# A fused delta-rule layer with feed-forward: the third slot's order, the place of the solve, and the engine of an add

## The reference, cut to what matters

```python
k = l2norm(silu(x @ Wk)); q = silu(x @ Wq); v = silu(x @ Wv)
log_f = log_sigmoid(x @ Wf1 @ Wf2); beta = sigmoid(x @ Wbeta) * 2.0
k_ = -beta[..., None] * k
# two steps a token: a decay step with (k_ * exp(log_f), k), and a write step with (k_, k, v, q)
def step(S, inp):
    g, a_t, b_t, k_t, v_t, q_t = inp
    bS = jnp.einsum('bhk,bhkv->bhv', b_t, S)
    S = jnp.exp(g)[..., None] * S + a_t[..., None] * bS[:, :, None, :] + k_t[..., None] * v_t[:, :, None, :]
    return (S, jnp.einsum('bhk,bhkv->bhv', q_t, S))
y = out * sigmoid(x @ Wog1 @ Wog2); y = y / sqrt(mean(y * y) + EPS) * norm_w   # per head
x = layernorm(x + y @ Wo)
x = layernorm(x + x @ W.T + b + x @ lilora_weight.T)
```

## Time and profile before

| | us |
|---|---|
| median of 3 runs | 2539.0 (2536.97 to 2541.99) |
| profiled execution | 2536.87, span 2535.0 |
| PE busy | 2121.5 (84%) |
| DVE busy | 1764.5 (70%) |
| ACT busy | 1627.2 (64%) |
| POOL busy | 838.3 (33%) |

### The profile page before, as it was taken

The page is one execution under the profiler, slowest core; times in us unless marked ns, Lnnn a source line. Parts: engine busy times, 40 slices in busy tenths (PEclk is TensorE's granted clock), DMA queues, the critical chain, the costliest instruction groups (busy, mean ns, idle before and its releaser), DMA issues.

```text
span 2535.0 us, 191611 instructions
## 1 busy us (share of the span) xinstructions
PE 2121.5 (84%) x85960; PEld 1591.0 (63%) x85960; DVE 1764.5 (70%) x4196; ACT 1627.2 (64%) x3048; POOL 838.3 (33%) x805
## 2 busy tenths in 40 slices
PE   6777888888888888888888888888888888889784
PEld 3556666666666666666666666666666666666573
DVE  3567567777766777766777766677876677776643
ACT  3656566666666666666666666666667666666554
POOL 1133233333333333323333323333333333332330
PEclk8889999999999999999999999999999999999886
DMA  3343244443344444344444344444334444433431
GB/s 100 85 120 113 90 132 136 139 130 98 120 130 139 133 129 121 105 123 138 137 131 131 96 124 136 131 139 128 111 117 124 137 137 132 130 98 120 131 111 38
DMA packets 558366, 305.46 MB, mean 120 GB/s; under 512 B 417186, under 2 KB 517152, under 8 KB 558240
## 3 DMA queue, kind: packets, MB, share of 16 engines
q1 hardware_dynamic: 558240, 304.19, 40.4%
HBM read 35.66 MB, written 16.78 MB: 21 GB/s over the span
## 4 chain that ended last, share of the span: by engine, by line
PE 57%; DVE 22%; issue 15%; ACT 5%; DMA 1%; SPq 0%; DVEq 0%; ACTq 0%
PE bank L582 15%; PE bank L716 8%; PE bank L741 7%; PE wide L724 7%; PE wide L732 4%; DVE uq_a L1162 4%; DVE inv L1166 4%; ACT t_t L890 3%; DVE dd L1248 3%; PE bank L655 3%; PE bank L614 2%; DVE change L1113 2%; PE bank L605 2%; PE bank L599 2%; DVE k_col L1267 2%
## 5 line engine op out<-in xcount | busy, mean ns | idle before, releaser
L475 POOL TENSOR_TENSOR state<-state,change 128x512 f32<-128x512 f32 x252 | 347.2, 1378 | 1354.2 <-DVE change L1113 1354.2
L582 PE MATMUL bank<-x_col,w_kqv 128*128 128x512 f32 x768 | 372.4, 622 | 55.9 <-issue 43.7
L741 PE MATMUL bank<-uq_now,s_now 32*32 32x24 f32 x32768 | 364.4, 187 | 9.0 <-issue 7.3
L741 PEld LDWEIGHTS bank<-uq_now,s_now 32*32 32x32 f32 x32768 | 350.4, 105 | 14.4 <-issue 10.2
L724 PE MATMUL wide<-wa_now,delta 32*32 32x80 f32 x16512 | 350.2, 234 | 3.2 <-ACT wa_now L874 2.5
L860 ACT ACTIVATE delta<-wide 128x256 f32<-128x256 f32 x256 | 98.1, 383 | 388.0 <-DVE change L1113 383.6
L1137 DVE COPY_PREDICATED aq<-ci,bank 128x128 f32<-128x128 int32 x256 | 77.3, 302 | 346.7 <-PE bank L716 218.3
L724 PEld LDWEIGHTS wide<-wa_now,delta 32*32 32x32 f32 x16512 | 308.3, 108 | 4.9 <-DMA wa_now<-aq 2.8
L479 POOL TENSOR_TENSOR state<-state,edge 128x512 f32<-128x512 f32 x252 | 292.7, 1161 | 19.8
L732 PEld LDWEIGHTS wide<-x_now,t_now 32*32 32x32 f32 x16448 | 174.0, 108 | 149.0 <-issue 148.6
L1105 DVE TENSOR_TENSOR o_col<-qs,wide 128x64 f32<-128x64 f32 x512 | 89.2, 215 | 252.2 <-PE wide L724 249.9
(11 more groups left out here) (96 smaller groups left out, 3827.4 us busy)
## 6 DMA issues: line engine op xcount, KB each, us to landing
s_now<-state SPq DMA_DIRECT2D x256, 256.0 KB
uq_now<-uqv SPq DMA_DIRECT2D x256, 192.0 KB
t_now<-t_t SPq DMA_DIRECT2D x256, 128.0 KB
uq_a<-uqv SPq DMA_DIRECT2D x64, 384.0 KB, 3.1
low<-uqv SPq DMA_DIRECT2D x64, 384.0 KB
x_col<-in_xt_dram SPq DMA_DIRECT2D x32, 512.0 KB, 3.9
w_a<-w_col SPq DMA_DIRECT2D x64, 256.0 KB, 3.7
inv<-w_col SPq DMA_DIRECT2D x64, 256.0 KB
```

Source lines behind the costliest of these rows:

```text
L475: pool.tensor_tensor(mine, mine, change[m % 2][:, :, :, :].rearrange("p m b v -> p (m b) v"), ALU.add).then_inc(s_added.handle, 1)
L582: mm = pe.matmul(ps[:, :], w_kqv[:, a, w, f * P:(f + 1) * P], x_col[:, a, :], start=a == 0, stop=a == KT - 1)
L741: mm = pe.matmul(p1_bank[quarter(h), m, b, :], s_now[quarter(h), m, b, :], uq_of(uq_now, m % HF)[quarter(h), m // HF, b * RQ:(b + 1) * RQ] ...
```

## The change

Seven edits, made together:

- TensorE turns the scores first in the third slot and projects k behind them; `FILLS` has `nt` ahead of `k`.
- ScalarE copies the scores into `low` first and takes k's silu behind them.
- VectorE does the solve's steps 1 to 7 at the end of the third slot and 8 to 15 at the end of the fourth; the fifth keeps the decay's floor alone.
- VectorE turns `w_row` between the last two pairs of masked copies in the second slot instead of in the third.
- ScalarE copies the inverse into `both` at the end of the fifth slot instead of the sixth.
- VectorE adds the old state to `change` in place, right behind the transposes.
- GpSimd only multiplies: `change` times the decay, into `state`.

```diff
--- before.py
+++ after.py
@@ -103,7 +103,7 @@
               "q": (2, HF), "beta": (2, HF), "f": (2, HF), "yss": (-1, HF), "kss": (2, HF), "nt": (1, 4),
               "wo": (-1, TT // 2), "tt": (1, 4)}
     PER_BANK = {s: GB if s == "nt" else 1 for s in STAGES}
-    FILLS = [(s, i) for some in ("v", "gate", "small", "k", "nt", "q", "ht", ("beta", "f"), "ff", "yss", "kss", "wo", "tt")
+    FILLS = [(s, i) for some in ("v", "gate", "small", "nt", "k", "q", "ht", ("beta", "f"), "ff", "yss", "kss", "wo", "tt")
              for i in range(2) for s in ((some,) if isinstance(some, str) else some)
              if i < (1 if s in ("beta", "f") else STAGES[s][1])]
     RING = 3
@@ -471,12 +471,10 @@
                 if m == QC:
                     pool.wait_ge(edge_ready.handle, edge_ready.at(g + 1, HF))
                 mine = state[:, qc, :, :, :].rearrange("p m b v -> p (m b) v")
-                pool.wait_ge(s_turned.handle, s_turned.at(g, m + 1))
-                pool.tensor_tensor(mine, mine, change[m % 2][:, :, :, :].rearrange("p m b v -> p (m b) v"),
-                                   ALU.add).then_inc(s_added.handle, 1)
+                moved = change[m % 2][:, :, :, :].rearrange("p m b v -> p (m b) v")
                 pool.wait_ge(s_added.handle, s_added.at(g, m + 1))
                 decay = edge[own][:, blk, qc * QI:(qc + 1) * QI, :, :].rearrange("p q f b -> p (q f b)")
-                pool.tensor_tensor(mine, mine, decay.unsqueeze(2).to_broadcast([P, CT * GB, HD]),
+                pool.tensor_tensor(mine, moved, decay.unsqueeze(2).to_broadcast([P, CT * GB, HD]),
                                    ALU.mult).then_inc(state_ready.handle, 1)
 
             def iteration(j, c):
@@ -656,11 +654,11 @@
                     mm.then_inc(filled["small"].handle, 1)
 
             def dense2(j):
-                if there(j + 2):
-                    for f in range(HF):
-                        project(j, "k", 0, f)
                 if there(j + 1):
                     turn_scores(j)
+                if there(j + 2):
+                    for f in range(HF):
+                        project(j, "k", 0, f)
 
             def dense3(j):
                 if there(j + 2):
@@ -977,10 +975,6 @@
                     act.activation(inv[:, :, :, :], cf[:, C_EYE:C_EYE + ROWS * ROWS].rearrange(
                         "p (i j) -> p i j", i=ROWS).unsqueeze(2).to_broadcast([P, ROWS, HPH, ROWS]),
                                    ACT.Copy).then_inc(inv_set.handle, 1)
-                if front:
-                    for f in range(HF):
-                        act.wait_ge(filled["k"].handle, filled["k"].at(j + 2, f + 1))
-                        act.activation(k_col[:, f, :], bank("k", f)[:, :], ACT.Silu).then_inc(drained["k"].handle, 1)
                 if next_one:
                     for k in range(4):
                         act.wait_ge(filled["nt"].handle, filled["nt"].at(j + 1, k + 1))
@@ -989,6 +983,10 @@
                             half = slice(b * TILES, (b + 1) * TILES)
                             act.activation(low[half, 4 * k:4 * k + 4, :, :], src[half, :, :, b, :], ACT.Copy,
                                            scale=-1.0).then_inc(drained["nt"].handle, 1)
+                if front:
+                    for f in range(HF):
+                        act.wait_ge(filled["k"].handle, filled["k"].at(j + 2, f + 1))
+                        act.activation(k_col[:, f, :], bank("k", f)[:, :], ACT.Silu).then_inc(drained["k"].handle, 1)
 
                 scan_part(3)
                 query(3)
@@ -1026,6 +1024,11 @@
                     act.wait_ge(e_floored.handle, e_floored.at(j + 2, 1))
                     act.activation(dd[:, :, :, 1:SLOTS], dd[:, :, :, 1:SLOTS], ACT.Ln,
                                    bias=one).then_inc(f_logged.handle, 1)
+                if next_one:
+                    act.wait_ge(solve_step.handle, solve_step.at(j + 1, 2 * (ROWS - 1)))
+                    for b in range(GB):
+                        half = slice(b * TILES, (b + 1) * TILES)
+                        act.activation(both[half, :, :, b, :], inv[half, :, :, :], ACT.Copy).then_inc(inv_spread.handle, 1)
 
                 scan_part(5)
                 query(5)
@@ -1044,11 +1047,6 @@
                                        bias=eps_l2).then_inc(drained["kss"].handle, 1)
                     act.wait_ge(drained["kss"].handle, drained["kss"].at(j + 2, HF))
                     act.activation(ss_col[:, :, :], ss_col[:, :, :], ACT.Exp, scale=-0.5).then_inc(r_ready.handle, 1)
-                if next_one:
-                    act.wait_ge(solve_step.handle, solve_step.at(j + 1, 2 * (ROWS - 1)))
-                    for b in range(GB):
-                        half = slice(b * TILES, (b + 1) * TILES)
-                        act.activation(both[half, :, :, b, :], inv[half, :, :, :], ACT.Copy).then_inc(inv_spread.handle, 1)
 
                 scan_part(6)
                 query(6)
@@ -1112,6 +1110,12 @@
                 for f in range(HF):
                     last = dve.transpose(dst[:, f, :, :], up_bank[:, f, :, 0:GB * HD])
                 last.then_inc(s_turned.handle, 1)
+                if isinstance(g, int) and g == G - 1 and blk == 1:
+                    return
+                dve.wait_ge(s_turned.handle, s_turned.at(g, m + 1))
+                moved = change[m % 2][:, :, :, :].rearrange("p m b v -> p (m b v)")
+                dve.tensor_tensor(moved, moved, state[:, qc, :, :, :].rearrange("p m b v -> p (m b v)"),
+                                  ALU.add).then_inc(s_added.handle, 1)
 
             def turn_right_sides(j, c, n):
 
@@ -1202,33 +1206,30 @@
                 turn_part(1)
                 if next_one:
                     mask_pair(j + 1, 1 - c, 2)
-                    mask_pair(j + 1, 1 - c, 3)
-
-                scan_part(2)
-                turn_part(2)
-                if next_one:
                     for i in range(2):
                         some = slice(i * TILES // 2, (i + 1) * TILES // 2)
                         last = dve.transpose(w_row[1 - c][:, some, :], w_col[:, some, :])
                     last.then_inc(w_turned.handle, 1)
+                    mask_pair(j + 1, 1 - c, 3)
+
+                scan_part(2)
+                turn_part(2)
+                if next_one:
+                    dve.wait_ge(inv_set.handle, inv_set.at(j + 1, 1))
+                    dve.wait_ge(drained["nt"].handle, drained["nt"].at(j + 1, 4 * GB))
+                    solve(j + 1, 0, 7)
 
                 scan_part(3)
                 turn_part(3)
                 if next_one:
-                    dve.wait_ge(inv_set.handle, inv_set.at(j + 1, 1))
-                    dve.wait_ge(drained["nt"].handle, drained["nt"].at(j + 1, 4 * GB))
-                    solve(j + 1, 0, 8)
+                    solve(j + 1, 7, ROWS - 1)
 
                 scan_part(4)
                 turn_part(4)
-                if next_one:
-                    solve(j + 1, 8, 11)
                 if front:
                     dve.wait_ge(drained["f"].handle, drained["f"].at(j + 2, HF))
                     dve.tensor_scalar(dd[:, :, :, 1:SLOTS], dd[:, :, :, 1:SLOTS], MAX_FALL, None,
                                       ALU.min).then_inc(e_floored.handle, 1)
-                if next_one:
-                    solve(j + 1, 11, ROWS - 1)
 
                 scan_part(5)
                 turn_part(5)
```

More of the change, by code:

```diff
@@ L658, in dense2 @@
             def dense2(j):
+                if there(j + 1):
+                    turn_scores(j)
                 if there(j + 2):
@@ L661, in dense2 @@
                         project(j, "k", 0, f)
-                if there(j + 1):
-                    turn_scores(j)
             def dense3(j):
@@ L1204, in iteration @@
                     mask_pair(j + 1, 1 - c, 2)
+                    for i in range(2):
+                        some = slice(i * TILES // 2, (i + 1) * TILES // 2)
+                        last = dve.transpose(w_row[1 - c][:, some, :], w_col[:, some, :])
+                    last.then_inc(w_turned.handle, 1)
                     mask_pair(j + 1, 1 - c, 3)
@@ L1209, in iteration @@
                 if next_one:
-                    for i in range(2):
-                        some = slice(i * TILES // 2, (i + 1) * TILES // 2)
-                        last = dve.transpose(w_row[1 - c][:, some, :], w_col[:, some, :])
-                    last.then_inc(w_turned.handle, 1)
+                    dve.wait_ge(inv_set.handle, inv_set.at(j + 1, 1))
+                    dve.wait_ge(drained["nt"].handle, drained["nt"].at(j + 1, 4 * GB))
+                    solve(j + 1, 0, 7)
                 scan_part(3)
```

## The result

The changed kernel takes 2687.0 us (median of 4 runs, 2679.8 to 2695.1) against 2538.3 us before: a ratio of 1.058, 95% interval 1.055 to 1.062. The direction was forecast; the size was not. 2596 us was predicted, 2550 to 2650 the range. The profiled execution has a span of 2678.0 us, 143 us more than before, at a mean granted clock of 0.919 instead of 0.960.

A forecast was written before the change was run, and what follows sets the result against it. No single engine bounds: VectorE waits for TensorE in the first four slots, the reverse from the sixth. 1.45 + 2.0 - 2.2 + 0.1 gives 1.4 us a group, 42 us, plus 15 for the clock: 2596 us, range 2550 to 2650.

The forecast's parts named there:

- The chain of the fourth slot: Fourth slot: solve steps ahead of the update make x_now 4.2 us later and stall TensorE 2.9 us at h's transposes.
- the ring's wait: Fourth slot, ring of three banks: the second half of h's transposes waits for q's first bank to be drained, 2.9 us.
- The third slot: Third slot, transposes first: the second k bank needs the first transposed bank emptied; no stall, 0.1 us booked.
- The add: VectorE, slots six to eight: adding the old state costs 2.0 us a group; GpSimd's shorter work gives 2.2 us back.
- Rival B: Late slots: GpSimd's lighter load gives nothing back, so the 2.2 us stay; 2662 us, chance 0.12.
- The clock: TensorE's granted clock: half of the stalls cost a 1.5 us dip, fewer boundary dips; 0.5 us a group, 15 us.
- The rest of the sum: All terms but TensorE's clock: 1.45 + 2.0 - 2.2 + 0.1, rounded up to 1.4 us a group, 42 us over 30 groups.
- the cover in the sixth slot: Sixth slot: VectorE comes 1.69 us late to finished updates, so earlier TensorE stalls cost only what exceeds that.
- The range: Whole kernel: 2550 to 2650 us, from the forecast and the nearer part of the rival in which GpSimd gives nothing back.
- Rival A: Fourth to sixth slot: stall under 1.7 us is covered; without one, 1.6 us a group gained, 2491 us; chance 0.11.

## Why the prediction was right in its mechanism and wrong in its size

- **The chain of the fourth slot** held to a tenth: x_now 4.1 us later against its slot than before (6.22 us behind the end of the updates instead of 2.08; 4.2 forecast), a stall of 2.84 us (2.9), at the transposes of h, in each group. The runs with 3, 4, 5 and 7 steps and the one without the order and the add (3.68 against 3.7) bear it out, and the run with q drained first shows that the ring's wait alone turns the late update into lost time.
- **The third slot** cost the 0.1 us that was booked: from the start of its `deltas` to those of the fourth are 9.30 instead of 9.24 us. Another 0.2 us were lost between the group's first scores and the third slot (16.74 instead of 16.50 us), where the prediction booked nothing; why is open.
- **The add** was right: 2.0 us against 2.2 given back was forecast; the kernel with the add alone gained 0.2 us a group. A net gain does not test the two terms, but the operations do. Between the profile before and that of the add alone, the late slots' four scans go from 874 to 731 ns each, the four products with kb_col from 870 to 736, the two with q_col from 768 to 678, k's from 1735 to 1591 and kb's from 1877 to 1226: 2.1 us a group. The add takes 703 ns, 2.1 us in three slots. Left out of the forecast: the solve gains too, where it met GpSimd (its products of 252 elements go from 804 to 603 ns, the sums from 786 to 422). In the profile of the changed kernel, by form between 400 and 2300 us:

```profile
L1117 DVE TENSOR_TENSOR change<-change,state 128x512 f32<-128x512 f32 x191 | 132.2, 692 | 6.6
...
L489 POOL TENSOR_TENSOR h_row<-h_row,bias_row 128x256 f32<-128x256 f32 x96 | 83.2, 885 | 34.5 <-DVE inv L1170 21.9 <-PE bank L622 12.6
...
L1268 DVE TENSOR_TENSOR k_col<-k_col,ss_col 128x1024 f32<-128x1024 f32 x24 | 38.2, 1591 | 0.0
...
L1272 DVE SCALAR_TENSOR_TENSOR kb_col<-kb_col,k_col 128x1024 f32<-128x1024 f32 x24 | 29.4, 1226 | 2.7
```

  The add takes 0.69 us. k's product fell from 1735 to 1591 ns and kb's from 1877 to 1226. Rival B is refuted.
- **The clock** is the step that failed. "Taking half of the stalls to cost a dip of 1.5 us and a few boundary dips less, I add 0.5 us a group". Measured: a fall of the clock at every one of the 28 stalls, 3.0 us a group and 90 us in all. The group of 80.4 us shows where: 1.8 us in the expansion of beta and f, 1.0 in the fifth slot's scan work (4.83 us from its start to the feed-forward instead of 3.82). The price of a dip came from "a group with such a dip is 2.0 us longer", but that group, 1077.06 to 1153.58, has two falls of 3.4 us each, and TensorE is at work in both:

```profile
1081.40:1084.80 3.40, 3.40 (x112) 2.72 (x99) 1.04 (x5) 1.78 (x5) 0.00 (x0) 0.50 0.65 204
1132.60:1136.00 3.40, 3.40 (x5) 1.30 (x4) 3.37 (x6) 2.77 (x4) 0.67 (x1) 0.50 0.01 2
```

  So by these two groups one fall of 3.4 us costs about 1.0 us, less than was taken. What was wrong is how many stalls bring a fall (all, not half) and how long it is (6.8 us or more in 27 of 28). The upper end that was named, 1.9 us a group, was too low for the same reason.
- **The rest of the sum** was 16 us too low. Without the clock's term the prediction's own sum was 2581 us, and the kernel with the stall filled by three matmuls took 2597. The 91 us between 2596 and 2687 are these 16 and the 75 by which 90 us of clock exceed the 15 booked. The 16 are not taken apart, but the starts of the `deltas` point at the cover in the sixth slot. The group of 80.4 us against that of 74.5: 0.2 us less up to the third slot, 0.1 more in the third, 4.8 more in the fourth, 1.0 more in the fifth, 0.9 less in the sixth, 1.1 more from the seventh to the end of the group, where the clock falls a second time (1210.9 to 1214.3). The sixth slot gave TensorE 0.9 us back, where 1.69 was booked.
- **The range** was too narrow even by its own bounds: add, stall and clock at their upper ends together make some 4.4 us a group, 2671 us, not 2650. The 2687 measured lies beyond both.
- **Rival A** was right that a short stall leaves a gain: with three steps ahead the kernel gains 33 us. Its bound of 1.7 us was not: with five steps the stall is 1.06 us and the kernel 41 us slower. Where the clock did not fall behind that stall a group took 74.5 us, no more than before the change; where it fell, up to 78.6.

## What to carry to other kernels

- A piece of work that is moved ahead of a wait is not free because its engine was idle there. Count what stands behind it in the queue of the second engine: here ScalarE's drains of banks, which TensorE needed two pieces later. The slack of that chain (1.3 us) gave the step count that pays.
- A new stall of TensorE costs its own length and then the time at 1.2 GHz behind it: here 2.8 us of waiting cost 3.0 us more. Price it with the dense work that follows the stall, not with a dip seen elsewhere. Filling a stall with matmuls that nobody reads tells the two apart, if the filling is timed first; so does a comparison, within one execution, of groups where the clock fell with groups where it did not.
- Taking work off GpSimd can be worth VectorE's time for it where the two meet in SBUF.

## What the runs showed of the hardware that was not expected

- Short waits of TensorE in a busy stretch brought its granted clock down to 0.50, and not always for the same time. With waits of about 1.07 us (five steps ahead) this happened behind 17 of 28, for 3.4 to 10.2 us; with 2.84 us (the changed kernel) at all 28, for 6.8 us or more in 27; with 3.68 us (the solve alone) at all 28, for 10.2 us in 24 and 6.8 us in 4. With waits of 0.2 us the mean clock was that of the kernel before (0.961 and 0.960). What decides whether it falls behind a wait of 1.07 us is open.
- VectorE's and GpSimd's operations with two SBUF inputs took turns where GpSimd's bias adds fell into the solve. Two operations of 240 elements, the first beside a bias add and the second not:

```profile
1176.37 0.82 DVE L1166 TENSOR_TENSOR uq_a<-low,inv 128x240 f32<-128x240 f32 x1
...
1177.22 0.41 DVE L1170 TENSOR_TENSOR inv<-inv,uq_a 128x240 f32<-128x240 f32 x1
```

  0.82 against 0.41 us, and the bias adds took 885 ns on average instead of 726. That agrees with the Trainium skill's SBUF — State Buffer (section on its two separate sides), which has whichever of the two starts first hold the shared ports for the whole instruction; the solve's eight steps took 8.2 us, 1.9 over the 6.3 of the forecast, hidden in the changed kernel and not in the one with q drained first.
- A 128x512 float32 matmul is two instructions and 0.86 us of TensorE; I had taken it for half of that from the time of one.
